# Second attention of a small language model tower: one sequence of 128 units, with the next batch's projections placed between them

## The reference

```
q = hidden_states @ w_q          # 128 -> 8 heads x 64, no bias
k = hidden_states @ w_k
v = hidden_states @ w_v
s = jnp.einsum('qhd,khd->qhk', qch / sqrt(64), kch, precision=HIGHEST)
e = jnp.exp(s - max(s)) ; out = einsum('khf,qhk->qhf', vch, e) / e.sum()
return attn @ w_out + b_out      # 512 -> 128, added to h
```

## Time and profile before

| | us |
|---|---|
| median of 3 runs (lowest, highest) | 1368.13 (1366.05, 1370.78) |
| the profiled execution's own time | 1377.66 |
| its span, first to last instruction | 1375.9 |
| PE busy, DVE busy, ACT busy, POOL busy | 1090.5, 1043.6, 688.7, 483.3 |

### The profile page before, as it was taken

The page is one execution under the profiler, slowest core; times in us unless marked ns, Lnnn a source line. Parts: engine busy times, 40 slices in busy tenths (PEclk is TensorE's granted clock), DMA queues, the critical chain, the costliest instruction groups (busy, mean ns, idle before and its releaser), DMA issues.

```text
span 1375.9 us, 24081 instructions
## 1 busy us (share of the span) xinstructions
PE 1090.5 (79%) x7848; PEld 835.0 (61%) x7848; DVE 1043.6 (76%) x3087; ACT 688.7 (50%) x1457; POOL 483.3 (35%) x402
## 2 busy tenths in 40 slices
PE   2288585785964798788898878789899898969998
PEld 2255454554643778776787778556565565656675
DVE  3577695776928999999999999288586776845587
ACT  1366584665813344333343433177485675825433
POOL 7354372543710243224322434245162442620000
PEclk9789698997987889999999999899999999988999
DMA  3210000000000000000000001200000000000000
GB/s 79 69 72 1 0 0 0 0 0 0 1 31 1 1 2 2 1 2 1 2 1 2 2 1 40 77 1 1 0 0 0 0 0 0 1 1 1 1 8 23
DMA packets 6425, 14.63 MB, mean 11 GB/s; under 512 B 1855, under 2 KB 4482, under 8 KB 5762
## 3 DMA queue, kind: packets, MB, share of 16 engines
q1 hardware_dynamic: 5314, 11.42, 2.4%
q0 software_dynamic: 1024, 2.10, 0.6%
HBM read 12.47 MB, written 1.05 MB: 10 GB/s over the span
## 4 chain that ended last, share of the span: by engine, by line
DVE 34%; issue 31%; PE 24%; POOL 5%; DVEq 3%; ACT 3%; DMA 0%; POOLq 0%; SPq 0%; ACTq 0%
DVE one_u L897 5%; DVE w_v L891 5%; PE quad L1070 4%; DVE a_eT L694 4%; DVE i L829 3%; PE quad L1322 3%; PE bank L1317 3%; PE quad L1082 3%; POOL wu L345 2%; DVE vals L906 2%; DVE m L822 2%; DVE bi L845 2%; POOL a_en L363 1%; DVE one_v L888 1%; DVE a_negmax L681 1%
## 5 line engine op out<-in xcount | busy, mean ns | idle before, releaser
L363 POOL TENSOR_TENSOR a_en<-a_e,a_rrec 128x512 f32<-128x512 f32 x256 | 265.2, 1040 | 302.6 <-DVE a_rrec L688 292.5
L395 POOL TENSOR_TENSOR vals<-relu_in,g_sb 128x512 f32<-128x512 f32 x80 | 145.3, 1844 | 316.3 <-ACT g_sb L554 290.6
L681 DVE TENSOR_REDUCE a_negmax<-bank 128x1 f32<-128x512 f32 x256 | 175.9, 690 | 41.7 <-PE bank L1268 25.3
L427 ACT ACTIVATE a_e<-bank,a_negmax 128x512 f32<-128x512 f32 x256 | 176.0, 688 | 61.9 <-DVE a_negmax L681 51.1
L1070 PE MATMUL quad<-ident,a_en 128*128 128x128 f32 x1024 | 163.9, 284 | 44.0 <-DVE a_eT L694 36.6
L1070 PEld LDWEIGHTS quad<-ident,a_en 128*128 128x128 f32 x1024 | 110.0, 143 | 136.7 <-issue 120.5
L694 DVE TENSOR_TENSOR a_eT<-quad,a_eT 128x512 fp32r<-128x512 f32 x256 | 172.3, 675 | 4.5 <-ACT a_eT L436 4.2
L1082 PE MATMUL quad<-a_eT,a_v 128*128 128x512 f32 x512 | 174.2, 431 | 1.0 <-DVE a_eT L694 0.9
L436 ACT CAST a_eT<-quad 128x512 fp32r<-128x512 f32 x256 | 147.8, 577 | 15.2 <-PE quad L1070 15.2
L1210 PE MATMUL bank<-xnT,wd 128*128 128x128 f32 x1024 | 129.1, 286 | 4.9 <-ACT relu_in L521 4.9
L1210 PEld LDWEIGHTS bank<-xnT,wd 128*128 128x128 f32 x1024 | 123.2, 197 | 8.7 <-ACT relu_in L521 7.8
(11 more groups left out here) (207 smaller groups left out, 1818.5 us busy)
## 6 DMA issues: line engine op xcount, KB each, us to landing
wd<-in_pk_down SPq DMA_DIRECT2D x1, 2048.0 KB, 8.2
wu<-in_pk_up SPq DMA_DIRECT2D x1, 2048.0 KB, 13.2
wu<-in_moe_w SPq DMA_DIRECT2D x2, 1024.0 KB
out<-h SPq DMA_DIRECT2D x4, 256.0 KB, 2.3
wd<-in_num_rows SPq DMA_DIRECT2D x1, 512.0 KB
vals<-in_pk_wqT SPq DMA_DIRECT2D x1, 512.0 KB
vals<-in_pk_keys SPq DMA_DIRECT2D x1, 512.0 KB
wd<-in_a_wq SPq DMA_DIRECT2D x1, 512.0 KB
```

What stands on the lines that cost most here:

```text
L363: nc.gpsimd.tensor_tensor(m.en[:, s % 3, :], m.e[:, s % 3, :], m.rrec[:, s % 4:s % 4 + 1].to_broadcast([P, S]), ALU.mult).then_inc(a.nr, 1)
L395: nc.gpsimd.tensor_tensor(*weigh_args(t, c, k, g_sb[:, slot, :])).then_inc(vals_pool, 1)
L427: nc.scalar.activation(m.e[:, s % 3, :], bank[LOGITS[s % 3]][:, :], ACT.Exp, bias=m.negmax[:, s % 4:s % 4 + 1], accum_out=m.rowsum[:, s % ...
L681: V.tensor_reduce(m.negmax[:, s % 4:s % 4 + 1], bank[LOGITS[s % 3]][:, :], AX.X, ALU.max, negate=True).then_inc(a.mx, 1)
```

## The change

`heads1`, `attention(a1, ...)` and the loop over batches are replaced by one sequence of NU1 = 128 units on each engine, written out. A label L from 0 to 63 says when a piece of batch n's preparation is done: during unit L of batch n-1 (L < 32) or unit L - 32 of batch n itself. `uses_at(L)` puts the q projection of head x at L = 9 + 4x, the k projection at 11 + 4x, v tile x at 19 + 4x; layer norm is at L = 1, 4 and 7. Labels below 32 of batch 0 stand ahead of the first unit (16 projections). The q and k buffers are single: head x of the next batch overwrites head x of this one as soon as its four units have made their logits. v and the result `oT1` are doubled. The projections use PSUM banks 5 and 7. The output projection of the batch before stands in units 9 to 12, a quarter in each, and its addition to `h` in unit 13. The PV chunks of a head are dealt differently over the steps, on one accumulator (bank 4), and `outT1` stands in another step. The output weights are loaded with the other weights into space of `wd`.

```diff
+        def uses_at(L):
+            found = []
+            if L >= 9 and (L - 9) % 4 == 0 and (L - 9) // 4 < H:
+                found.append(("q", (L - 9) // 4))
+            if L >= 11 and (L - 11) % 4 == 0 and (L - 11) // 4 < H:
+                found.append(("k", (L - 11) // 4))
+            if L >= 19 and (L - 19) % 4 == 0 and (L - 19) // 4 < TPB:
+                found.append(("v", (L - 19) // 4))
+            return found
...
+            sp.dma_start(wo1, a1_wo.rearrange("p (h d) -> p h d", h=H)).then_inc(ld_a1, 16)
             sp.wait_ge(ffn_add, NT)
-            sp.dma_start(wo1[:], a1_wo.rearrange("p (h d) -> p h d", h=H)).then_inc(ld_wo1, 16)
...
+            def heads1_act(n, L):
...
+                for kind, x in uses_at(L):
+                    u = order1[n, kind, x]
+                    act.wait_ge(p1_ps, u + 1)
+                    src = bank[bank1[u]][:, :]
+                    if kind == "q":
+                        if n:
+                            act.wait_ge(a1.qk, (n - 1) * UNITS + TPB * (x + 1))
+                        nc.scalar.mul(qT1[:, x, :], src, SCALE1).then_inc(p1_hi, 1)
...
+            def expT_hi1(s):
+                hd, j = s // TPB, s % TPB
+                act.wait_ge(a1.tr, s + 1)
+                if j == 0 and hd >= 2:
+                    act.wait_ge(a1.pv, TPB * (hd - 1))
...
+            for s in range(NU1 + 8):
+                if s < NU1:
+                    exp1(s)
+                if 0 <= s - 3 < NU1:
+                    expT_hi1(s - 3)
+                if s >= 11 and (s - 11) % TPB == 0:
+                    outT1((s - 11) // TPB)
+                b, L = s // UNITS, s % UNITS
+                if b < B and L + UNITS < 2 * UNITS:
+                    heads1_act(b, L + UNITS)
+                if b + 1 < B:
+                    heads1_act(b + 1, L)
...
+            for s in range(NU1 + 4):
+                if s < NU1:
+                    rowmax1(s)
+                if 0 <= s - 1 < NU1:
+                    invert1(s - 1)
+                if 0 <= s - 4 < NU1:
+                    expT_lo1(s - 4)
+                b, L = s // UNITS, s % UNITS
+                if b < B and L + UNITS < 2 * UNITS:
+                    heads1_dve(b, L + UNITS)
+                if b + 1 < B:
+                    heads1_dve(b + 1, L)
+                if L == 13 and b:
+                    residual1(b - 1)
...
+            for s in range(NU1 + 9):
+                if s < NU1:
+                    logits1(s)
+                if 0 <= s - 3 < NU1:
+                    expT1(s - 3)
+                if s >= 10 and (s - 10) // TPB < NU1 // TPB:
+                    for c in ((0,), (1, 2), (3,), ())[(s - 10) % TPB]:
+                        pv1((s - 10) // TPB, c)
+                b, L = s // UNITS, s % UNITS
+                if b < B and L + UNITS < 2 * UNITS:
+                    heads1_pe(b, L + UNITS)
+                if b + 1 < B:
+                    heads1_pe(b + 1, L)
+                if 9 <= L < 9 + TPB and b:
+                    project1(b - 1, L - 9)
```

More of the change, by code:

```diff
@@ L68, in tower @@
         ones = sb("ones", [P, P])
-        mhalf = sb("mhalf", [P, TPB * H])
+        small = sb("small", [P, 3, TPB])
+        mhalf, veps, rstd = [small[:, n, :] for n in range(3)]
         phalf = sb("phalf", [P, TPB * H])
@@ new lines, in _ @@
+            for L in range(UNITS):
+                heads1_act(0, L)
+            for s in range(NU1 + 8):
[10 more added lines that the diff above has]
+                    heads1_act(b + 1, L)
@@ L952, in _, with heads1_dve @@
             dve.drain()
-            def heads1(b, before=None):
-                for n in range(2 * H + TPB):
-                    if n == 2 * H and before is not None:
-                        residual(a1, before)
-                    dve.wait_ge(p1_hi, b * (2 * H + TPB) + n + 1)
-                    src = bank[n % 4][:, :]
-                    if n < H:
-                        half = mD.qT[DH1:P, n, :]
-                        V.scalar_tensor_tensor(half, src[DH1:P, :], a1.scale, half.bitcast(F32),
+            def heads1_dve(n, L):
+                if L == 1:
+                    ln_stats(lnD, n * TPB, TPB)
+                if L == 4:
+                    if n:
+                        dve.wait_ge(lnD.ps, n)
+                    ln_scale(lnD, n, n * TPB, TPB)
+                for kind, x in uses_at(L):
+                    u = order1[n, kind, x]
+                    dve.wait_ge(p1_hi, u + 1)
+                    src = bank[bank1[u]][:, :]
+                    if kind == "q":
+                        half = qT1[DH1:P, x, :]
+                        V.scalar_tensor_tensor(half, src[DH1:P, :], SCALE1, half.bitcast(F32),
@@ new lines, in pv1 @@
+            def pv1(g, c):
+                b, hd = g // H, g % H
+                if c == 0:
+                    pe.wait_ge(a1.lo, TPB * (g + 1))
+                    if hd == 0:
+                        pe.wait_ge(p1_lo, order1[b, "v", TPB - 1] + 1)
+                    if g:
+                        pe.wait_ge(a1.ots, g)
+                for part in range(2):
+                    last = mm(bank[4], v1[:, b % 2, c, hd, :], eT1[:, hd % 2, part, c, :],
+                              start=(c == 0 and part == 0), stop=(c == TPB - 1 and part == 1))
+                last.then_inc(a1.pv, 1)
@@ new lines, in project1 @@
+            def project1(b, j):
+                if j == 0:
+                    pe.wait_ge(a1.ots, H * (b + 1))
+                    pe.wait_ge(p1_lo, order1[b, "k", H - 1] + 1)
+                dst = bank[5][:, j * D:(j + 1) * D]
+                for g in range(H):
+                    mm(dst, oT1[:, b % 2, g, j * P:(j + 1) * P], wo1[:, g, :], start=(g == 0), stop=False)
+                last = mm(dst, ones[0:1, :], bo1[:], start=False, stop=True)
+                if j == TPB - 1:
+                    last.then_inc(a1.proj, 1)
@@ new lines, in heads1_pe @@
+            def heads1_pe(n, L):
+                if L == 7:
+                    if n:
+                        pe.wait_ge(p1_lo, order1[n - 1, "q", H - 1] + 1)
+                    transpose_xn(lnD, n)
+                for kind, x in uses_at(L):
+                    u = order1[n, kind, x]
+                    if u == 0 or (kind, x) == ("q", 0):
+                        pe.wait_ge(lnD.sb, n + 1)
+                    if prev1[u] >= 0:
+                        pe.wait_ge(p1_lo, prev1[u] + 1)
+                    if kind == "k" and x == 1 and n >= 2:
+                        pe.wait_ge(a1.add, n - 1)
+                    if kind == "v":
+                        last = mm(bank[bank1[u]][:, :], xnT1[n % 2][:, x * P:(x + 1) * P], wv1, start=True, stop=True)
+                    else:
+                        w = (wq1 if kind == "q" else wk1)[:, x * P:(x + 1) * P]
+                        last = mm(bank[bank1[u]][:, :], w, xnT1[n % 2], start=True, stop=True)
@@ L1290, in heads1 @@
                     last.then_inc(p1_ps, 1)
-                pe.wait_ge(p1_lo, (b + 1) * (2 * H + TPB))
-            transpose_xn(lnD, 0)
-            heads1(0)
-            with pe.Fori(0, B - 1) as b:
-                attention(a1, b, logits1, lnD)
-                heads1(b + 1, b)
-            attention(a1, B - 1, logits1)
-            project1(B - 1)
+            pe.wait_ge(ld_a1, 80)
+            for L in range(UNITS):
+                heads1_pe(0, L)
+            pe.wait_ge(p1_lo, first1)
@@ L1302, in _ @@
+            for j in range(TPB):
+                project1(B - 1, j)
             pe.wait_ge(ld_moe, 80)
```

162 lines of the change are left out of this document (106 added, 56 removed).

## The result

The changed kernel took 1489.95 us (median of 4 runs, 1486.19 to 1493.83); the kernel before took 1368.17 us on the same chip (4 runs, 1366.05 to 1370.78). The ratio is 1.089, 95% interval 1.087 to 1.091: 121.8 us slower. The forecast was 1500. The profiled execution took 1489.92 us.

The account below looks back on a forecast made before the run. No engine's sum was taken as the bound, but the second attention's chain of waits between PE, ACT and DVE: 1368 + 109 (net, longer chain) + 25 (PE's clock) = 1502, rounded to 1500 us; range 1440 to 1570.

Parts of the forecast that it names:

- B: Second unit of a head, with a q projection: becomes a round trip of 3.29 us where a plain unit takes 1.38.
- D: Fourth unit of a head, with a k projection: ACT waits for P V issued in the next unit; 6.51 us.
- D with v: A head's fourth unit with k and v projections: 0.86 us more on PE and 0.70 on DVE, 8.07 us.
- a plain head of batch 3: Last batch, head without projections: exp of its first unit starts 1.4 us late, so 7.6 us instead of 6.2.
- the ring: Second attention: DVE waits for ACT's copy, ACT for the next unit's P V; heads 12.6 us (v 14.1) against 6.2.
- The sum of the chain: Second attention: batches of 102.9, 115.5, 115.5 and 78.8 us, 412.7 against 300.4 now, +112.3.
- The clock: Second attention: idle time in each head lowers PE's clock, slowing part of its path in the fourth unit; +25 us.
- The head of the stage: Ahead of the second attention's first logits: only 16 of 20 projections stand there, -3.4 us.
- The distance between profile and median: Whole kernel: profiled execution took 9.5 us more than the median; the same distance taken for the changed kernel.
- Clock low throughout: Rival: PE's clock stays low through the merged stretch of the second attention, +132, 1609 us; chance 0.07.
- Light chain: Rival: in the second attention ACT loses no time to the next unit's P V; +30, 1398 us; chance 0.09.
- Faster, bound by the busiest engine: Rival: round trips overlap and PE sets a batch of the second attention, 71.3 against 83.7; about 1328 us; chance 0.06.

Follow-up runs that it names:

- both_moves: Changed kernel with DVE's low halves of the projections one unit later and a head's last P V chunk one unit earlier; 1372.89 us, ratio 0.997.
- filler: Changed kernel with six dummy products of 512 columns behind the logits of each head's second unit, in PE's idle stretch; 1490.31 us, ratio 1.081.
- low_later: Changed kernel with DVE's low halves of the projections one unit later, PE and ACT as in the change; 1404.26 us, ratio 1.019.
- pv_earlier: Changed kernel with the last P V chunk of a head one unit earlier on PE, low halves left in place; 1421.06 us, ratio 1.029.

## Why the prediction was right

**The place and the mechanism: right, shown.** Predicted and measured, in units of the trace: B 3.29, measured 3.22 at full clock; D 6.51, measured 6.29 or 6.30; D with v 8.07, measured 7.74 to 7.77; a plain head of batch 3 7.6, measured 7.48. The two edits of both_moves touch only the two waits of the ring that the prediction names, DVE's for ACT's copy and ACT's for the P V of the next unit, and give back all of the loss.

**The sum of the chain: right, 6 to 12 us too dear.** Batches of 102.9, 115.5, 115.5 and 78.8 us were forecast without the clock; measured with it they are 101.0, 120.2, 116.8 and 80.3 (row maxima of units 0, 32, 64 and 96 at 897.4, 998.4, 1118.63 and 1235.44, the last batch to 1.8 us behind 1313.93). Their sum is 418.3 where 412.7 and 25 for the clock make 437.7. Of the 19.4 us between them 7 to 13 are the clock's (next paragraph). A head at full clock is 12.2 us where I had 12.56, which is 10 us over 26 heads.

**The clock: right in sign, wrong in place, 7 to 13 us too large.** This step failed, though the forecast held: I let PE run at half clock "in D" and wrote of B that "PE is no hindrance here". The windows show the reverse. The clock falls behind the idle time, which ends with B's transposes. B then pays, since a q projection of 1.92 us is no longer ready when ACT comes to it, and the clock is back before D's path begins. From the feed-forward stage I had taken some 7 us for the rise; here it took about 4. The view of waits has ACT standing for the late q projection 14 times, 12.2 us in all. Over 23 units B (all but the first and the two with the output projection), what exceeds 3.23 us is 18.1 us; 5.1 of it is in two units that hold layer norm as well and 1.2 in two that hold the addition to `h`, which leaves 12. Unit 35, a D at low clock, and unit 41 pay too: each is 1.6 us longer than in filler. So it is 12 to 18 us where I had 25. The filler, which won 7 us in the units and 11 by the ratio, fits that size. The Trainium skill ("TensorE: Matmul & The Clock Gate", "Why this matters for your kernels") warns that gaps between bursts send the clock back to half. The rows agree that it falls (0.50 after 3.32 us of idle time), but not behind every gap: of 21 q projections with an idle time of 3.3 us or more ahead of B's transposes, 16 took 1.20 to 1.92 us and five 1.02 or 1.03, and the clock over 440 us was 0.90. "Almost always low", as I drew from it, did not come.

**What I left out: the drain, and the short first units of a batch before.** From the end of the last unit to the addition to `h` the changed kernel takes 19.0 us, the kernel before 16.8: +2.2. And the last batch of the kernel before took 47.4 us (first logits at 1158.70, end of its last unit at 1206.09), not the 49.4 that I added for it, because the first eight units of a batch follow each other faster (9.3 us instead of 12.4); from its first logits to the end of its last unit it has 298.4 us, where I had 300.4. In the changed kernel the same stretch has 419.1, where I had 437.7. With that the stage's sum closes: 137.3 forecast (112.3 and 25), - 18.6 + 2.0 + 2.2 = 122.9, as measured. Nothing is left over for the unrolled code, which I had put at nothing.

**The head of the stage: right.** From the end of the feed-forward stage to the first logits it is 24.05 us, before 27.62 (872.58 to 896.63, 880.07 to 907.69): 3.6 less where 3.4 was forecast.

**The distance between profile and median: wrong, and of no weight.** The profiled execution of before took 9.5 us more than the median, and I took the same distance for the changed kernel. It has none (1489.92 and 1489.95). The 7.5 us lay ahead of this stage, in work that the change doesn't touch. Since I forecast from the median by a difference of stages, it did not enter.

**The rivals.** "Clock low throughout" falls with the windows at 1.00 in D. "Light chain" falls with the 86.6 us that ACT waits for P V. "Faster, bound by the busiest engine" was wrong for this order of work but true of the idea: with the waits gone PE does set the pace. Its condition, ACT's copy without the wait for its own unit's row maximum, was not needed: the copy still waits for that, but DVE no longer stands for it ahead of the next row maximum. low_later, pv_earlier and a distance between uses of a bank make it so, and the result is 1348 where that rival had 1328.

## What to carry to other kernels

Laying one stage's work between another's units paid here only once no engine's list had an instruction that waits for something begun in the same unit. Write down for every hand-off in how many units it has to arrive, and put its consumer one unit later than that: here this alone (both_moves) moved the time from 1.089 to 0.997. Then do the same for buffers: two projections in one bank whose low halves come a unit late need more than two units between them (with two, PE stood 0.4 to 1.7 us in these kernels). When a move gives nothing, look for the wait that now stands first in the list of the engine that was freed. Here it was three times a projection waiting for its bank (rows of 1.73, 0.79 and 2.04 us), each time with everything else of PE queued behind it. Off the path such a wait costs nothing; at the head of the busiest engine's list it is paid in full.
